# Routing of a soft mixture of experts: layer norm's gamma and beta moved from GpSimd into VectorE's normalisation

## The chip, the cores and the metric

One core of one Trainium2 chip. The metric is the device time of one execution in microseconds, median over runs.

## What is computed

Two layers on `x` (16 batches of 256 rows of 256 numbers, fp32): attention over a context and a feed-forward part, then a second attention and a soft mixture of 16 experts with 16 slots each. The change lies in the last part only, in the front of it:

```
xn = _layernorm(x, ln_gamma, ln_beta)      # (x - mu) * rsqrt(var + LN_EPS) * gamma + beta
x_unit = _l2norm(xn, axis=-1)
mu_unit = _l2norm(mu, axis=0)
logits = jnp.einsum('bnd,des->bnes', x_unit * scale, mu_unit)
dispatch = jax.nn.softmax(logits, axis=1)
combine = jax.nn.softmax(logits.reshape(B, N, E * S), axis=-1).reshape(B, N, E, S)
slot_in = jnp.einsum('bnd,bnes->besd', xn, dispatch)
```

The experts work on `slot_in`, and `combine` mixes what they give back.

## The kernel before, in words

The kernel is a row of stages with a barrier of all engines between them: `prologue` (keys and values), `attention0`, `ffn`, `attention1`, and in `moe` the stages `route`, `experts` and `combine`. Everything around `route` is left as it is. Each engine has its own program, in which the order is written out by hand; they are tied by semaphores alone. There is no scheduler.

`route` holds a batch as 128 partitions x 2 chunks (`NC`) x 256. Its body runs 17 times, unrolled (`every_batch`), and each engine is at another batch, so that in iteration f the following is done.

- **VectorE** (`batch` at L1684): normalise batch f+3 (`ln.normalise`, L346: two tensor_scalar into `xn`, recorded at L351), first maxima `top` of the logits (L1670), `disp_lo` of batch f-1 (L1692), inverse of the exponentials' sum `rinv` (L1675), first two `weight` (L1681), two `xT_lo` (L1665), second maxima, statistics of batch f+4 (L331, L334), inverse length of f+2 (L1660), second `rinv` and `weight`.
- **GpSimd** (L1768): `split_x(f)`, which makes `xaS_lo` (L1765); `affine(f+3)`, which makes `xg` from `xn` and gamma (L1746) and `xa` from `xg` and beta (L1752); `lengths(f+2)` (L1758, L1761); `inverse_deviation(f+4)`, which makes `var_eps` and `rstd` (L340, L343).
- **ScalarE** (L1623): `unit(f+1)`, which scales two rows of `xa` into `xu` (L1602), `disp_hi` (L1630), first exponentials (L1614), `xT_hi` (L1608), `square(f+2)` (L1596), second exponentials, `round_x(f+1)` into `xaS_hi` (L1621), then the copies `comb` (L1643) and `slots` (L1645) of batch f-1.
- **TensorE** (L1561): first logits of f (L1538), transposes of the first `weight` of f-1 (L1547), transposes of `xu` of f+1 (L1528), second logits, transposes of the second `weight`, and `slot_inputs` of f-1 (L1557), which waits for `disp_lo` and `xaS_lo`.

Logits, weights and dispatch are fp32 split into a high and a low part (`_hi`, `_lo`). `xn`, `xg`, `xu` and the logits' banks exist once, `xa` three times (`XR = 3`, L1470), so `affine(f)` waits until `xu` and `xaS_lo` of batch f-3 have been made.

Ahead of the batches stands a start in which the vectors `mu` are normalised (`mu_sq`, `mu_diag`, `mu_unit`, `mu_hi`, `mu_lo`, L1709 to L1731), mixed with the normalisation of batches 0, 1 and 2. gamma, beta and the scale are loaded at the stage's beginning; `affine(0)` and `mu_diag` wait for them.

Of the kernel before, what the change touches and what calls it, by code (L numbers as in the profile page):

```python
# [19 lines left out]
ALU = mybir.AluOpType  # L20
# [6 lines left out]
P = 128  # L27
B = 16
N = 256
NC = N // P  # L30
D = 256
# [18 lines left out]
def at_least(eng, sem, value):  # L50

    if not isinstance(value, int) or value > 0:
        eng.wait_ge(sem, value)


def wait_apart(eng, sem, value):

    at_least(eng.engine, sem, value)
    if not isinstance(value, int):
        eng.engine.sem_inc(eng.ticks, 1)  # L64
# [244 lines left out]
def x_rows(st, b, q):  # L309

    return st.x[:, bass.ds(b, 1), q, :].rearrange("p b e -> p (b e)")
# [1136 lines left out]
def route(nc, d, st):  # L1448
# [7 lines left out]
    with ExitStack() as stack:  # L1456
        m = Memory(nc, stack, "route")
# [9 lines left out]
        half = m.sb("half", [P, NC])  # L1467
        ln = LayerNorm(nc, m, st)
        xg = m.sb("xg", [P, NC, D])
        XR = 3  # L1470
        xa = [m.sb(f"xa{i}", [P, NC, D]) for i in range(XR)]
        sq = m.sb("sq", [P, D])
        sumsq, length, length_min, inv_length = (m.sb(n, [P, NC]) for n in ("sumsq", "length", "length_min", "inv_length"))
# [14 lines left out]
        in_, expert_in = m.sem("small_in"), m.sem("expert_in")  # L1488
        const_ready, mu_step, mu_psum, mu_ready = m.sem("const_ready"), m.sem("mu_step"), m.sem("mu_psum"), m.sem("mu_ready")
        mu_pow = m.sem("mu_pow")  # L1490
        xg_ready, xa_ready, sumsq_ready = m.sem("xg_ready"), m.sem("xa_ready"), m.sem("sumsq_ready")
        len_ready, lmin_ready, inv_ready, xu_ready = m.sem("len_ready"), m.sem("lmin_ready"), m.sem("inv_ready"), m.sem("xu_ready")
        xas_hi, xas_ready = m.sem("xas_hi"), m.sem("xas_ready")
        xt_psum, xt_hi, xt_lo = m.sem("xt_psum"), m.sem("xt_hi"), m.sem("xt_lo")
# [7 lines left out]
        def every_batch(eng, body):  # L1502
            for f in range(B + 1):
                body(f)
# [83 lines left out]
        @block.scalar  # L1588
        def _(act):
            def square(f, i):  # L1590

                act.wait_ge(xa_ready, f + 1)
                for q in range(NC):
                    at_least(act, sumsq_ready, NC * f + q)
                    at_least(act, len_ready, f)
                    nc.scalar.activation(sq[:, :], xa[f % XR][:, q, :], ACT.Square, accum_out=sumsq[:, q:q + 1]).then_inc(sumsq_ready, 1)  # L1596

            def unit(f, i):
                act.wait_ge(inv_ready, f + 1)
                at_least(act, xt_psum, DC * f)  # L1600
                for q in range(NC):
                    nc.scalar.mul(xu[:, q, :], xa[f % XR][:, q, :], inv_length[:, q:q + 1]).then_inc(xu_ready, 1)  # L1602

            def transposed_x(f, i):
                for c in range(DC):
                    act.wait_ge(xt_psum, DC * f + c + 1)
                    at_least(act, l_psum, 2 * (f - 1))
                    nc.scalar.copy(xT[i][0][:, c, :], x_bank[c][:, 0:N]).then_inc(xt_hi, 1)  # L1608

            def exponentials(f, k):  # L1610
                act.wait_ge(top_ready, 2 * f + k + 1)
                at_least(act, weight_ready, 4 * (f - 1) + 2 * k + 2)
                for r in range(2):
                    nc.scalar.activation(ex[k][:, r, :], l_bank[k][:, r * ES:(r + 1) * ES], ACT.Exp,  # L1614
                                         bias=top[k][:, r:r + 1], accum_out=rsum[k][:, r:r + 1]).then_inc(ex_ready, 1)

            def round_x(f, i):

                at_least(act, i_psum, f - 1)
                act.wait_ge(xa_ready, f + 1)  # L1620
                nc.scalar.copy(xaS[i][0][:, :, :], xa[f % XR][:, :, :]).then_inc(xas_hi, 1)  # L1621

            def batch(f):  # L1623
                g = f - 1
                if f + 1 < B:
                    unit(f + 1, 0)
                if f > 0:
                    act.wait_ge(t_psum, 2 * g + 1)
                    at_least(act, i_psum, g)
                    nc.scalar.copy(disp[0][:, :, :], t_bank[0][:, :].rearrange("p (q n) -> p q n", q=NC)).then_inc(disp_hi, 1)  # L1630
                if f < B:
                    exponentials(f, 0)
                if f + 1 < B:
                    transposed_x(f + 1, (f + 1) % 2)
                if f + 2 < B:
                    square(f + 2, 0)
                if f < B:
                    exponentials(f, 1)
                if f + 1 < B:
                    round_x(f + 1, (f + 1) % 2)  # L1640
                if f > 0:
                    act.wait_ge(t_psum, 2 * g + 2)
                    nc.scalar.copy(st.comb[:, :, g, :], t_bank[1][:, :].rearrange("p (j n) -> p j n", j=EC)).then_inc(comb_stored, 1)  # L1643
                    act.wait_ge(i_psum, g + 1)
                    nc.scalar.copy(st.slots[:, :, g, :], i_bank[:, :].rearrange("p (c n) -> p c n", c=DC)).then_inc(slots_stored, 1)  # L1645

            square(0, 0)
            unit(0, 0)
            transposed_x(0, 0)
            square(1, 1)  # L1650
            round_x(0, 0)
            every_batch(act, batch)

        @block.vector
        def _(dve):
            def invert_length(f):

                dve.wait_ge(lmin_ready, f + 1)
                at_least(dve, xu_ready, NC * f)
                nc.vector.reciprocal(inv_length[:, :], length_min[:, :]).then_inc(inv_ready, 1)  # L1660
# [23 lines left out]
            def batch(f):  # L1684
                g = f - 1
                if f + 3 < B:
                    ln.normalise(dve, f + 3, xg_ready, 1)
                if f < B:
                    maxima(f, 0)
                if f > 0:  # L1690
                    dve.wait_ge(disp_hi, g + 1)
                    nc.vector.tensor_tensor(disp[1][:, :, :], t_bank[0][:, :].rearrange("p (q n) -> p q n", q=NC),  # L1692
                                            fp32_of(disp[0][:, :, :]), ALU.subtract).then_inc(disp_lo, 1)
                if f < B:
                    invert(f, 0)
                    weigh(f, 0)
                if f + 1 < B:
                    transposed_x(f + 1, (f + 1) % 2)
                if f < B:
                    maxima(f, 1)  # L1700
                if f + 4 < B:
                    ln.statistics(dve, f + 4)
                if f + 2 < B:
                    invert_length(f + 2)
                if f < B:
                    invert(f, 1)
                    weigh(f, 1)
# [2 lines left out]
            ln.statistics(dve, 0)  # L1710
            dve.wait_ge(mu_psum, 1)
            nc.vector.tensor_copy(mu_sum[:, :], i_bank[:, 0:EC]).then_inc(mu_step, 1)
            ln.normalise(dve, 0, xg_ready, 1)
            ln.statistics(dve, 1)

            dve.wait_ge(mu_pow, 2)
            nc.vector.reciprocal(mu_inv[:, :], mu_max[:, :]).then_inc(mu_step, 1)
            dve.wait_ge(mu_step, 3)
            dve.wait_ge(in_, 48)
            for j in range(EC):  # L1720
                last = nc.vector.tensor_scalar(mu_diag[:, j, :], st.ident[:, :], mu_inv[:, j:j + 1], scale[:, 0:1],
                                               ALU.mult, ALU.mult)
            last.then_inc(mu_step, 1)
            ln.normalise(dve, 1, xg_ready, 1)
            dve.wait_ge(mu_psum, 2)
            nc.vector.tensor_tensor(mu_unit[:, :, :], mu_raw[:, :, :], l_bank[0][:, 0:ES].unsqueeze(1).to_broadcast([P, DC, ES]),
                                    ALU.mult).then_inc(mu_step, 1)
# [4 lines left out]
            ln.statistics(dve, 2)  # L1732
            invert_length(0)
            transposed_x(0, 0)
            ln.normalise(dve, 2, xg_ready, 1)
            ln.statistics(dve, 3)
            invert_length(1)
            every_batch(dve, batch)
# [1 line left out]
        @block.gpsimd  # L1740
        def _(pool):
            poolt = Ticking(pool, m.sem("pool_ticks"))
            def affine(f, i):
                wait_apart(poolt, ln.ready, NC * f + NC)
                wait_apart(poolt, xa_ready, f)
                nc.gpsimd.tensor_tensor(xg[:, :, :], ln.xn[:, :, :], gamma[:, :].unsqueeze(1).to_broadcast([P, NC, D]),  # L1746
                                        ALU.mult).then_inc(xg_ready, 1)
                wait_apart(poolt, xg_ready, f + 1)

                wait_apart(poolt, xu_ready, NC * (f - 2))  # L1750
                wait_apart(poolt, xas_ready, f - 2)
                nc.gpsimd.tensor_tensor(xa[f % XR][:, :, :], xg[:, :, :], beta[:, :].unsqueeze(1).to_broadcast([P, NC, D]),  # L1752
                                        ALU.add).then_inc(xa_ready, 1)

            def lengths(f):
                wait_apart(poolt, sumsq_ready, NC * f + NC)
                wait_apart(poolt, lmin_ready, f)
# [10 lines left out]
            def batch(f):  # L1768
                if f < B:
                    split_x(f, f % 2)  # L1770
                if f + 3 < B:
                    affine(f + 3, 0)
                if f + 2 < B:
                    lengths(f + 2)
                if f + 4 < B:
                    ln.inverse_deviation(pool, f + 4)
# [6 lines left out]
            nc.gpsimd.tensor_tensor(mu_norm[:, :], mu_sum[:, :], half[:, 0:EC], ALU.pow).then_inc(mu_pow, 1)  # L1783
            wait_apart(poolt, mu_pow, 1)
            nc.gpsimd.tensor_scalar(mu_max[:, :], mu_norm[:, :], NORM_EPS, None, ALU.max).then_inc(mu_pow, 1)
            wait_apart(poolt, in_, 48)
            affine(0, 0)
            ln.inverse_deviation(pool, 1)
            lengths(0)
            affine(1, 1)  # L1790
            lengths(1)
            ln.inverse_deviation(pool, 2)
            affine(2, 0)
            ln.inverse_deviation(pool, 3)
            every_batch(pool, batch)

# [338 lines left out]
```

## Time and profile before

| | |
|---|---|
| median of 3 runs | 1199.65 us (1196.87, 1199.65, 1201.66) |
| the profiled execution | 1201.5 us, its span 1199.7 us |
| busy over the span | TensorE 1020.2 us (85%), VectorE 883.1 (74%), ScalarE 751.3 (63%), GpSimd 470.3 (39%) |
| `route` in the span | from about 957 to 1110 us |

Busy shares over the whole span mix stages with different limits. The rows further down come from the stretch of `route`; times there are microseconds from the span's first instruction, and a row's columns are start, length, engine, line, operation, what is written and from what, its shape and count; in brackets stands how long the engine had been idle before it and who ended that.

### The profile page before, as it was taken

How to read it: one execution, taken by the hardware profiler on the slowest of the kernel's cores; microseconds unless marked ns; L12 is line 12 of the kernel's file. 1: busy time of each engine (PE TensorE's matmuls, PEld its weight loads, DVE VectorE, ACT ScalarE, POOL GpSimd, SP SyncE). 2: the span in 40 equal slices, each digit the busy share in tenths (PEclk: the TensorE clock that was granted, in tenths of full speed). 3: DMA queues.
4: the chain of work that ended last, by engine and by line, in shares of the span. 5: the costliest groups of instructions: out<-in, count | busy, mean ns of one | idle time of the engine just before them, and what ended most of it. 6: DMA issues, size and time to landing. Idle time of an engine off the chain costs nothing. (4 is left out here: it accounts for less than half of the span.)

```text
span 1199.7 us, 27786 instructions
## 1 busy us (share of the span) xinstructions
PE 1020.2 (85%) x8021; PEld 977.4 (81%) x8021; DVE 883.1 (74%) x2261; ACT 751.3 (63%) x2515; POOL 470.3 (39%) x801
## 2 busy tenths in 40 slices
PE   6779999999999999799999947888888637777578
PEld 6679999999999998699999946787887627677567
DVE  3567767777776676677777747999998668986776
ACT  3467666666666666433333338999898527777774
POOL 0132232322323222112121126667676467663655
PEclk9889999999999999899999966999999959999789
DMA  7678970000000000100000035555556050000003
GB/s 216 152 134 218 145 122 0 0 0 0 0 0 0 0 0 1 32 1 0 0 0 0 0 109 150 154 157 164 154 152 171 13 110 2 1 2 1 1 18 122
DMA packets 72190, 75.04 MB, mean 63 GB/s; under 512 B 22608, under 2 KB 64436, under 8 KB 71988
## 3 DMA queue, kind: packets, MB, share of 16 engines
q1 hardware_dynamic: 71300, 73.52, 24.8%
q10 hardware_dynamic: 816, 0.66, 0.2%
q8 instruction: 32, 0.52, 0.2%
q14 instruction: 42, 0.34, 0.1%
HBM read 42.58 MB, written 31.54 MB: 62 GB/s over the span
## 5 line engine op out<-in xcount | busy, mean ns | idle before, releaser
L776 POOL TENSOR_TENSOR att_prob<-att_ex,att_rinv 128x308 f32<-128x308 f32 x128 | 89.9, 702 | 215.8 <-DVE att_rinv L679 202.4
L1059 ACT ACTIVATE att_ex<-att_s_bank,att_mx 128x77 f32<-128x77 f32 x512 | 143.1, 340 | 13.7 <-DVE att_mx L1127 12.2
L1346 ACT ACTIVATE ffn_hid<-ffn_h_bank,ffn_b 128x256 f32<-128x256 f32 x128 | 60.6, 474 | 125.3 <-DVE ffn_hT_lo L1377 65.3
L638 ACT ACTIVATE att_ex<-att_s_bank,att_mx 128x77 f32<-128x77 f32 x512 | 124.7, 332 | 11.5 <-DVE att_mx L669 11.4
L646 ACT ACTIVATE att_qT<-att_q_bank 128x256 f32<-128x256 f32 x128 | 49.1, 384 | 101.2 <-PE att_q_bank L496 100.2
L702 DVE TENSOR_TENSOR att_pT_lo<-att_t_bank,att_pT_hi 128x512 fp32r<-128x512 f32 x128 | 88.3, 690 | 32.2 <-ACT att_pT_hi L616 31.8
L1203 POOL TENSOR_TENSOR att_prob<-att_ex,att_rinv 128x256 f32<-128x256 f32 x128 | 79.8, 623 | 77.2 <-DVE att_rinv L1142 77.1
L516 PE MATMUL att_s_bank<-att_keys,att_qT 128*128 128x154 f32 x512 | 94.9, 308 | 0.0
L616 ACT CAST att_pT_hi<-att_t_bank 128x512 fp32r<-128x512 f32 x128 | 74.9, 586 | 24.4 <-PE att_t_bank L526 19.3
L540 PE MATMUL att_o_bank<-att_pT_hi,att_vals_hi 128*128 128x256 f32 x256 | 83.0, 324 | 3.0 <-DVE att_oT_lo L683 2.0
L967 PE MATMUL att_s_bank<-att_ks,att_qs 100*128 100x154 f32 x256 | 53.2, 292 | 34.3 <-ACT att_ex L1059 17.4
L1317 PE MATMUL ffn_o_bank<-ffn_w_hi,ffn_hT_hi 128*128 128x256 f32 x256 | 74.3, 290 | 7.8 <-DVE ffn_hT_lo L1377 7.8
L683 DVE TENSOR_TENSOR att_oT_lo<-att_o_bank,att_oT_hi 128x256 fp32r<-128x256 f32 x128 | 54.3, 424 | 33.1 <-ACT att_oT_hi L651 29.6
L496 PE MATMUL att_q_bank<-att_xT_hi,att_wq_hi 128*128 128x256 f32 x256 | 75.6, 295 | 2.9 <-DVE att_xT_lo L662 2.9
L526 PE MATMUL att_t_bank<-all_ident,att_prob 128*128 128x128 f32 x512 | 76.5, 272 | 0.0
L1304 PE MATMUL ffn_h_bank<-ffn_xT_hi,ffn_w_hi 128*128 128x256 f32 x256 | 72.6, 283 | 3.5 <-DVE ffn_xT_lo L1364 3.5
L967 PEld LDWEIGHTS att_s_bank<-att_ks,att_qs 100*128 100x128 f32 x256 | 42.1, 205 | 40.4 <-DMA att_qs<-q_dram 31.2
L1127 DVE TENSOR_REDUCE att_mx<-att_s_bank 128x4 f32<-128x308 f32 x128 | 59.7, 466 | 20.3 <-PE att_s_bank L967 20.2
L516 PEld LDWEIGHTS att_s_bank<-att_keys,att_qT 128*128 128x128 f32 x512 | 73.2, 193 | 1.0
L496 PE MATMUL att_q_bank<-att_xT_hi,att_wq_lo 128*128 128x256 f32 x256 | 73.4, 287 | 0.0
L496 PE MATMUL att_q_bank<-att_xT_lo,att_wq_hi 128*128 128x256 f32 x256 | 73.1, 286 | 0.0
L1304 PE MATMUL ffn_h_bank<-ffn_xT_lo,ffn_w_hi 128*128 128x256 f32 x256 | 72.2, 282 | 0.0
(274 smaller groups left out, 4141.3 us busy)
## 6 DMA issues: line engine op xcount, KB each, us to landing
att_qs<-q_dram SPq DMA_DIRECT2D x96, 128.0 KB, 2.8
ks_dram<-att_zeros SPq DMA_DIRECT2D x16, 462.0 KB, 5.7
att_ks<-ks_dram SPq DMA_DIRECT2D x16, 462.0 KB, 4.9
all_x<-in_x SPq DMA_DIRECT2D x4, 1024.0 KB, 7.5
att_vd<-vd_dram SPq DMA_DIRECT2D x16, 256.0 KB
q_dram<-att_qT_hi SPq DMA_DIRECT2D x16, 256.0 KB, 2.1
q_dram<-att_qT_lo SPq DMA_DIRECT2D x16, 256.0 KB, 2.1
out<-comb_y SPq DMA_DIRECT2D x16, 256.0 KB, 2.1
```

Source lines behind the costliest of these rows:

```text
L496: last = nc.tensor.matmul(q_bank[c % 2][:, 0:N], wq[a][:, k, c * P:(c + 1) * P], xT[b][:, k, :], start=n == 0, stop=n == 5)
L516: last = nc.tensor.matmul(out, qT[c % 2][:, q * P:(q + 1) * P], keys[:, kc, h0:h0 + 2, :], start=first, stop=True)
L526: last = nc.tensor.transpose(t_bank[t % 2][:, h * N + q * P:h * N + (q + 1) * P], prob[:, q, (2 * t + h) * SK:(2 * t + h) * SK + P], st.id ...
L540: last = nc.tensor.matmul(o_bank[j % 2][:, 0:N], vals[a][:, v * P:(v + 1) * P], pT[t % 2][b][:, h * N:(h + 1) * N], start=t % PC == 0 and ...
L616: nc.scalar.copy(pT[t % 2][0][:, :], t_bank[t % 2][:, :]).then_inc(pt_hi, 1)
L638: last = nc.scalar.activation(ex[t % RING][:, r, :], s_bank[t % 2][:, r * SK:(r + 1) * SK], ACT.Exp, bias=mx[t % 2][:, r:r + 1])
L702: nc.vector.tensor_tensor(pT[t % 2][1][:, :], t_bank[t % 2][:, :], fp32_of(pT[t % 2][0][:, :]), ALU.subtract).then_inc(pt_lo, 1)
L776: nc.gpsimd.tensor_tensor(out, e, w, ALU.mult).then_inc(p_ready, 1)
L967: last = nc.tensor.matmul(s_bank[t % 2][:, q * PAIR:(q + 1) * PAIR], qs[i][0:ROWS, t, q * P:(q + 1) * P], ks[i][0:ROWS, t // 4, t % 4, :, ...
L1059: last = nc.scalar.activation(ex[t % RING][:, r, :], s_bank[t % 2][:, r * SK:(r + 1) * SK], ACT.Exp, bias=mx[t % 2][:, r:r + 1], **total)
L1203: nc.gpsimd.tensor_tensor(main, e[:, :, :, 0:MAIN], w.to_broadcast([P, NC, 2, MAIN]), ALU.mult).then_inc(p_ready, 1)
L1304: last = nc.tensor.matmul(h_bank[t % 4][:, 0:N], w1[a][:, k, t, :], xT[b][:, k, :], start=n == 0, stop=n == 5)
```

## The change

`affine` goes from GpSimd's program, and with it the semaphore `xa_ready`. VectorE's `ln.normalise` is replaced in this stage by a local `normalise`: for each chunk one scalar_tensor_tensor (x - mean) * gamma into `xg`, and then for each chunk a second, xg * rstd + beta, into `xa`. Who waited for `xa_ready` now waits for `ln.ready`, which the second one raises. `xa` has four buffers instead of three, so `normalise(f)` waits for `xu` and `xaS_lo` of batch f-4, where `affine(f)` waited for those of f-3. In ScalarE's program `unit` moves from the head of an iteration, for batch f+1, to behind `round_x`, for batch f+2, ahead of the copies `comb` and `slots`. VectorE now waits for gamma, beta and the scale before `normalise(0)`.

```
-        XR = 3
+        XR = 4
...
-                act.wait_ge(xa_ready, f + 1)
+                act.wait_ge(ln.ready, NC * f + NC)
...
             def batch(f):
                 g = f - 1
-                if f + 1 < B:
-                    unit(f + 1, 0)
...
                     round_x(f + 1, (f + 1) % 2)
+                if f + 2 < B:
+                    unit(f + 2, 0)
...
             round_x(0, 0)
+            unit(1, 0)
...
+            def normalise(f):
+                dve.wait_ge(ln.rstd_ready, f + 1)
+                at_least(dve, ln.ready, NC * f)
+                for q in range(NC):
+                    nc.vector.scalar_tensor_tensor(xg[:, q, :], x_rows(st, f, q), ln.mean_var[:, q, 0:1], gamma[:, :],
+                                                   ALU.subtract, ALU.mult).then_inc(xg_ready, 1)
+                at_least(dve, xu_ready, NC * (f - XR + 1))
+                at_least(dve, xas_ready, f - XR + 1)
+                for q in range(NC):
+                    dve.wait_ge(xg_ready, NC * f + q + 1)
+                    nc.vector.scalar_tensor_tensor(xa[f % XR][:, q, :], xg[:, q, :], ln.rstd[:, q:q + 1], beta[:, :],
+                                                   ALU.mult, ALU.add).then_inc(ln.ready, 1)
...
-                    ln.normalise(dve, f + 3, xg_ready, 1)
+                    normalise(f + 3)
...
-            ln.normalise(dve, 0, xg_ready, 1)
+            dve.wait_ge(in_, 48)
+            normalise(0)
...
-            def affine(f, i):
-                wait_apart(poolt, ln.ready, NC * f + NC)
-                wait_apart(poolt, xa_ready, f)
-                nc.gpsimd.tensor_tensor(xg[:, :, :], ln.xn[:, :, :], gamma[:, :].unsqueeze(1).to_broadcast([P, NC, D]),
-                                        ALU.mult).then_inc(xg_ready, 1)
-                wait_apart(poolt, xg_ready, f + 1)
-
-                wait_apart(poolt, xu_ready, NC * (f - 2))
-                wait_apart(poolt, xas_ready, f - 2)
-                nc.gpsimd.tensor_tensor(xa[f % XR][:, :, :], xg[:, :, :], beta[:, :].unsqueeze(1).to_broadcast([P, NC, D]),
-                                        ALU.add).then_inc(xa_ready, 1)
```

How the order moves, first on VectorE, from one `weight` pair over the normalisation to the next batch's `xT_lo`. Before:

```order
L1681 TENSOR_SCALAR route_weight<-route_ex,route_rinv 128x256 x2
L351 TENSOR_SCALAR route_xn<-all_x,route_mean_var,route_rstd 128x256 x2
L1670 TENSOR_REDUCE route_top<-route_l_bank 128x2
L1692 TENSOR_TENSOR route_disp_lo<-route_t_bank,route_disp_hi 128x512
L1675 RECIPROCAL route_rinv<-route_rsum 128x2
```

And changed:

```order
L1695 TENSOR_SCALAR route_weight<-route_ex,route_rinv 128x256 x2
L1661 SCALAR_TENSOR_TENSOR route_xg<-all_x,route_mean_var,route_gamma 128x256 x2
L1667 SCALAR_TENSOR_TENSOR route_xa<-route_xg,route_rstd,route_beta 128x256 x2
L1684 TENSOR_REDUCE route_top<-route_l_bank 128x2
L1706 TENSOR_TENSOR route_disp_lo<-route_t_bank,route_disp_hi 128x512
L1689 RECIPROCAL route_rinv<-route_rsum 128x2
```

Two instructions have become four, at the same place. On GpSimd, one iteration from `rstd` to the next `rstd`, before:

```order
L343 TENSOR_TENSOR route_rstd<-route_var_eps,all_minus_half 128x2
L1765 TENSOR_TENSOR route_xaS_lo<-route_xa,route_xaS_hi 128x512
L1746 TENSOR_TENSOR route_xg<-route_xn,route_gamma 128x512
L1752 TENSOR_TENSOR route_xa<-route_xg,route_beta 128x512
L1758 TENSOR_TENSOR route_length<-route_sumsq,route_half 128x2
L1761 TENSOR_SCALAR route_length_min<-route_length 128x2
L340 TENSOR_SCALAR route_var_eps<-route_mean_var 128x2
```

And changed:

```order
L343 TENSOR_TENSOR route_rstd<-route_var_eps,all_minus_half 128x2
L1767 TENSOR_TENSOR route_xaS_lo<-route_xa,route_xaS_hi 128x512
L1760 TENSOR_TENSOR route_length<-route_sumsq,route_half 128x2
L1763 TENSOR_SCALAR route_length_min<-route_length 128x2
L340 TENSOR_SCALAR route_var_eps<-route_mean_var 128x2
```

The two products and sums with gamma and beta are gone; `xaS_lo` stays right behind `rstd`. On ScalarE, from the second exponentials of an iteration to the first of the next, before:

```order
L1614 ACTIVATE route_ex,route_rsum<-route_l_bank,route_top 128x256 x2
L1621 CAST route_xaS_hi<-route_xa 128x512
L1643 COPY moe_comb<-route_t_bank 128x2x256
L1645 COPY moe_slots<-route_i_bank 128x2x256
L1602 ACTIVATE route_xu<-route_xa,route_inv_length 128x256 x2
L1630 CAST route_disp_hi<-route_t_bank 128x512
```

And changed:

```order
L1614 ACTIVATE route_ex,route_rsum<-route_l_bank,route_top 128x256 x2
L1621 CAST route_xaS_hi<-route_xa 128x512
L1602 ACTIVATE route_xu<-route_xa,route_inv_length 128x256 x2
L1643 COPY moe_comb<-route_t_bank 128x2x256
L1645 COPY moe_slots<-route_i_bank 128x2x256
L1628 CAST route_disp_hi<-route_t_bank 128x512
```

`xu` of the same batch now comes ahead of two copies instead of behind them.

## Rows read from the trace of the kernel before

**Rows 1.** Stretch 984 to 1081 us: length, then busy us (instructions), clock, DMA

```profile
984.00:1081.00 97.00, 69.46 (x547) 64.54 (x547) 86.50 (x216) 73.78 (x238) 67.90 (x84) 0.98 0.01 1
```

**Rows 2.** Who waited for whom, 990 to 1079 us: total, times, longest

```profile
ACT route_ex L1614 <- DVE route_top L1670: 20.2, 22, 1.3
PE route_x_bank L1528 <- ACT route_xu L1602: 18.1, 10, 1.8
```

**Rows 3.** Order in time, VectorE: one batch, and `top` of batches 0 and 12

```profile
984.08 0.68 DVE L1670 TENSOR_REDUCE route_top<-route_l_bank 128x2 f32<-128x512 f32 x1
...
1023.01 1.59 DVE L351 TENSOR_SCALAR route_xn<-all_x,route_mean_var,route_rstd 128x256 f32<-128x256 f32 x2
...
1024.52 0.68 DVE L1670 TENSOR_REDUCE route_top<-route_l_bank 128x2 f32<-128x512 f32 x1
...
1026.29 0.17 DVE L1675 RECIPROCAL route_rinv<-route_rsum 128x2 f32<-128x2 f32 x1 [0.49 <-ACT route_ex L1614]
...
1026.49 1.27 DVE L1681 TENSOR_SCALAR route_weight<-route_ex,route_rinv 128x256 f32<-128x256 f32 x2
...
1027.67 0.75 DVE L1665 TENSOR_TENSOR route_xT_lo<-route_x_bank,route_xT_hi 128x256 fp32r<-128x256 f32 x2
...
1028.34 0.68 DVE L1670 TENSOR_REDUCE route_top<-route_l_bank 128x2 f32<-128x512 f32 x1
...
1081.21 0.68 DVE L1670 TENSOR_REDUCE route_top<-route_l_bank 128x2 f32<-128x512 f32 x1
```

**Rows 4.** Order in time, GpSimd, the same batch

```profile
1022.18 0.79 POOL L343 TENSOR_TENSOR route_rstd<-route_var_eps,all_minus_half 128x2 f32<-128x2 f32 x1
1022.86 1.27 POOL L1765 TENSOR_TENSOR route_xaS_lo<-route_xa,route_xaS_hi 128x512 fp32r<-128x512 f32 x1
...
1026.05 1.29 POOL L1752 TENSOR_TENSOR route_xa<-route_xg,route_beta 128x512 f32<-128x512 f32 x1
```

**Rows 5.** Order in time, VectorE, near the stage's end

```profile
1089.54 0.69 DVE L1692 TENSOR_TENSOR route_disp_lo<-route_t_bank,route_disp_hi 128x512 fp32r<-128x512 f32 x1 [1.35 <-ACT route_disp_hi L1630]
...
1090.66 0.62 DVE L1681 TENSOR_SCALAR route_weight<-route_ex,route_rinv 128x256 f32<-128x256 f32 x2
1091.19 0.75 DVE L1665 TENSOR_TENSOR route_xT_lo<-route_x_bank,route_xT_hi 128x256 fp32r<-128x256 f32 x2
```

**Rows 6.** Order in time, the start: VectorE's `mu` and GpSimd's `xa`

```profile
957.09 0.69 DVE L1709 TENSOR_TENSOR route_mu_sq<-all_raw 128x512 f32<-128x512 f32 x1 [1.01 <-PEq L98]
...
968.56 1.22 DVE L1729 CAST route_mu_hi<-route_mu_unit 128x512 fp32r<-128x512 f32 x1
969.57 1.32 POOL L1752 TENSOR_TENSOR route_xa<-route_xg,route_beta 128x512 f32<-128x512 f32 x1
969.81 1.63 DVE L1731 TENSOR_TENSOR route_mu_lo<-route_mu_unit,route_mu_hi 128x512 fp32r<-128x512 f32 x1
```

**Rows 7.** VectorE: two rows of the prologue; by line, ns min/median/max, first and last

```profile
8.96 0.76 DVE L275 SCALAR_TENSOR_TENSOR pro_wk_lo<-pro_w_raw,pro_wk_hi 128x256 fp32r<-128x256 f32 x2 [0.24 <-ACT pro_wk_hi L240]
9.64 0.89 DVE L278 TENSOR_TENSOR pro_wv_lo<-pro_w_raw,pro_wv_hi 128x128 fp32r<-128x128 f32 x2
...
L1373 DVE CAST ffn_hT_hi<-ffn_hid x128: 263/293/1254, 502.0 to 695.4; 128x256 fp32r<-128x256 f32 x128
...
L1681 DVE TENSOR_SCALAR route_weight<-route_ex,route_rinv x64: 340/352/1003, 986.0 to 1106.3; 128x256 f32<-128x256 f32 x64
...
L351 DVE TENSOR_SCALAR route_xn<-all_x,route_mean_var,route_rstd x32: 399/410/1357, 959.8 to 1080.9; 128x256 f32<-128x256 f32 x32
```

**Rows 8.** Order in time, the start: VectorE and, last, GpSimd

```profile
963.49 2.65 DVE L1721 TENSOR_SCALAR route_mu_diag<-all_ident,route_mu_inv,route_scale 128x128 f32<-128x128 f32 x2 [1.91 <-DMA route_scale<-in_L_ffn_scale]
967.20 0.74 DVE L351 TENSOR_SCALAR route_xn<-all_x,route_mean_var,route_rstd 128x256 f32<-128x256 f32 x2 [1.05 <-POOL route_rstd L343]
...
979.49 0.30 DVE L334 BATCH_NORM_AGGREGATE route_mean_var<-route_stats 128x2 f32<-128x6 f32 x2
...
981.44 0.22 POOL L340 TENSOR_SCALAR route_var_eps<-route_mean_var 128x2 f32<-128x2 f32 x1
```

More of the change, by code:

```diff
@@ L1490, in route @@
         mu_pow = m.sem("mu_pow")
-        xg_ready, xa_ready, sumsq_ready = m.sem("xg_ready"), m.sem("xa_ready"), m.sem("sumsq_ready")
+        xg_ready, sumsq_ready = m.sem("xg_ready"), m.sem("sumsq_ready")
         len_ready, lmin_ready, inv_ready, xu_ready = m.sem("len_ready"), m.sem("lmin_ready"), m.sem("inv_ready"), m.sem("xu_ready")
@@ L1619, in round_x @@
                 at_least(act, i_psum, f - 1)
-                act.wait_ge(xa_ready, f + 1)
+                act.wait_ge(ln.ready, NC * f + NC)
                 nc.scalar.copy(xaS[i][0][:, :, :], xa[f % XR][:, :, :]).then_inc(xas_hi, 1)
@@ L1718, in _ @@
             dve.wait_ge(mu_step, 3)
-            dve.wait_ge(in_, 48)
             for j in range(EC):
@@ L1723, in _ @@
             last.then_inc(mu_step, 1)
-            ln.normalise(dve, 1, xg_ready, 1)
+            normalise(1)
             dve.wait_ge(mu_psum, 2)
@@ L1734, in _ @@
             transposed_x(0, 0)
-            ln.normalise(dve, 2, xg_ready, 1)
+            normalise(2)
             ln.statistics(dve, 3)
@@ L1770, in batch @@
                     split_x(f, f % 2)
-                if f + 3 < B:
-                    affine(f + 3, 0)
                 if f + 2 < B:
@@ L1785, in _ @@
             nc.gpsimd.tensor_scalar(mu_max[:, :], mu_norm[:, :], NORM_EPS, None, ALU.max).then_inc(mu_pow, 1)
-            wait_apart(poolt, in_, 48)
-            affine(0, 0)
             ln.inverse_deviation(pool, 1)
             lengths(0)
-            affine(1, 1)
             lengths(1)
             ln.inverse_deviation(pool, 2)
-            affine(2, 0)
             ln.inverse_deviation(pool, 3)
```

## The prediction

> **What bounds the kernel now.** Only the routing stage is touched, and the first view to read is the table of stretches: from 984 to 1081 us, while twelve batches go by, VectorE is busy 86.50 of 97.00 us, TensorE 69.46, ScalarE 73.78 and GpSimd 67.90, at a granted clock of 0.98 [rows 1]. The highest share is only a hint. The second view, who waited for whom in 990 to 1079 us, shows which engine the others wait for: TensorE waits 18.1 us for `xu` in 10 waits of up to 1.8, ScalarE 20.2 us for VectorE's maxima in 22 [rows 2]. The third, VectorE's order in time, gives the verdict. A batch takes (1081.21 - 984.08) / 12 = 8.09 us, and in the batch shown VectorE goes from one instruction to the next with one idle piece of any size, 0.49 us before `rinv`, which waits for ScalarE's exponentials of the maxima that VectorE has just made [rows 3]. No maximum waits for TensorE. So a batch lasts as long as VectorE's instructions from start to start, and TensorE's wait for `xu` is slack.
>
> Two of VectorE's spacings are longer than the work in them. The two `xn` begin at 1023.01, but `top` only at 1024.52; GpSimd's `xaS_lo` runs from 1022.86 to 1024.13 [rows 3, 4]. The first pair of `weight` begins at 1026.49 and `xT_lo` at 1027.67, 1.18 later; GpSimd's `xa` runs from 1026.05 to 1027.34 [rows 3, 4]. Without a large GpSimd instruction beside it the same pair takes 1091.19 - 1090.66 = 0.53 us [rows 5]. In both places VectorE comes second and stands until GpSimd is through.
>
> **The sum, per batch.** Three edits matter.
>
> (1) GpSimd's two 128x512 instructions (`xg`, and `xa` of 1.29 us [rows 4]) go. GpSimd's own time is not on the path. What is on it is the collision of `xa` with `weight`: 1.18 - 0.53 = 0.65 us less.
>
> (2) VectorE's two `xn` become four scalar_tensor_tensor of 128x256. The price of one: the two in the prologue begin at 8.96 and what follows them at 9.64, so 0.34 each, one lasting 0.42; their scalar is a constant [rows 7]. Here it is a column of 128 numbers. Among one-input instructions of 128x256 the median is 293 ns with no such scalar, 352 with one, 410 with two [rows 7], so I add 0.06: 0.40 from start to start (lower bound 0.34; the upper one is a rival below).
>
> Where they stand matters more. `normalise` waits for `rstd`, GpSimd's instruction right ahead of `xaS_lo`; `rstd` ends at 1022.97, `xn` starts at 1023.01, `xaS_lo` had started at 1022.86 [rows 3, 4]. The change keeps this order, so the first of the four again meets `xaS_lo`. Does an instruction with two SBUF inputs stand still too? `mu_lo` (128x512, two SBUF inputs) took 1.63 us beside GpSimd's `xa` and ended at 971.44, 0.55 after it; `mu_sq`, of the same shape, took 0.69 alone [rows 6]. So yes, and what comes after the block is about the work itself, 0.28 for 256 columns. From the end of `xaS_lo` to the start of `top` I get 0.28 + 3 x 0.40 - 0.08 (the next one starts that much before the last ends: `xT_lo` ends at 1028.42, `top` starts at 1028.34 [rows 3]) = 1.40 us. Before it is 1024.52 - 1024.13 = 0.39 [rows 3, 4]. That is 1.01 us more.
>
> (3) ScalarE scales `xu` of two batches on ahead of the `comb` and `slots` copies. TensorE gets it nearly a microsecond sooner, and I cost this at nothing: what hides it is VectorE, since no maximum waits for TensorE. Between the second exponentials of a batch and the first of the next ScalarE has the same five instructions in either order, and in mid-stage it then waits for `top` anyway [rows 2]. At the end of the stage, where ScalarE's chain is the path (VectorE waits 1.35 us for `disp_hi` [rows 5]), the count is again the same. If VectorE's cover were gone, the price would be that of rival B. The fourth buffer makes `normalise` wait only for batch f-1, done a batch ago: nothing.
>
> Net per batch: +1.01 - 0.65 = +0.36 us. Twelve batches lie between `top` of batch 0 and of batch 12: +4.3 us. The `weight` of batch 12 still saves its 0.65.
>
> **The start.** The chain up to `top` of batch 0 is serial. `normalise(0)` must now wait for gamma and beta, which come at about 963.5 (that is when `mu_diag` could start): four instructions with the wait for their end 1.7, statistics 1.0, `rstd` 1.1 give `normalise(1)` at 967.3, against 967.20 [rows 8]: +0.1. It takes 0.9 more than two `xn`. `mu_hi` (1.22, of which about 0.43 is work, by 293 ns for half the columns at two a cycle) and `mu_lo` (1.63 against 0.69) lose their collisions [rows 6, 7]: -1.7. `normalise(2)`: +0.9. `var_eps` of batch 3 starts at 981.44 though its statistics ended at 979.79, because `xg` and `xa` of batch 2 stand ahead [rows 8]: -1.6. `normalise(3)`: +1.0, as above. Sum -0.4 us.
>
> **Total:** 4.3 - 0.65 - 0.4 = +3.3 us. Those are rounded up; with 0.393 for 0.40 it is +3.0, which I take. The profiled execution took 1201.5 us (span 1199.7), so it would be 1204.5; it lies 1.85 above the median of the runs, 1199.65, so the forecast is **1202.6 us**, 0.25% more: no change. 0.5%, or 6 us, is about what a measurement of this kernel can tell from none.
>
> The sum is steep in one number: 36 of the instructions lie in the twelve periods and about 15 in the start, so 0.01 us on each is 0.5 us. At the lower bound of 0.34 the total is +0.3 us. The Trainium skill's "VectorE: DVE Perf Modes", section on the TRN2 errata, gives an SBUF instruction 58 + FD cycles of 0.96 GHz, 327 ns here; by that rule the sum would be about -0.4 us. The prologue's row has 0.34 from start to start and 0.42 for one, and the measurement decides.
>
> **Rivals.** *A, no collision.* Every collision that I used has a one-input instruction or a tensor_tensor in it; no row shows a scalar_tensor_tensor beside GpSimd. If it runs on, `top` starts 4 x 0.40 = 1.6 after the first, against 1.51 before: +0.1 - 0.65 = -0.55 a batch, 12 times, -1.0 more in the start: about -9 us, 1191. TensorE and ScalarE could follow (72% and 76% busy now [rows 1]). Against it: `mu_lo`. The skill's "SBUF — State Buffer", section on who interferes with whom, says that any VectorE instruction with two SBUF inputs contends with a GpSimd one that reads SBUF; `mu_lo` agrees. 9%.
>
> *B, TensorE's wait was the path.* If a batch turns on `xu`, putting it ahead of two copies (some 0.95 us) saves 0.95 in each of 14 batches: 1199.65 - 13 = 1186. Against it: `top` never waits for TensorE [rows 3]. 3%.
>
> *C, slower: each of the four costs its full length.* They wait on semaphores of their own engine (`xa` for `xg`). If each such wait empties VectorE, the spacing is 0.42 + 0.06 + 0.04 = 0.52 instead of 0.393: 51 x 0.127 = +6.5 us on top, 1209. It counts as slower from 0.46 on (3.0 + 51 x 0.06 = 6). For it: nothing here shows two-input instructions with a column scalar back to back. Against it: `xa` of a half waits for the instruction before the last one, which has ended by then. 13%.
>
> That the change does not do what it says is no case: the order of instructions shows all three moves.
>
> **Chances and range.** The forecast mechanism has 75%, A 9, B 3, C 13. Its own range is +0.3 to +3.0 us with the spread of the runs shown (1196.87 to 1201.66, -2.8 and +2.0), some 1197 to 1205. A tenth of each side is left out beyond: the range reaches towards A and into C, 1194.5 to 1208.5. The forecast case falls past +6 us in some 3 of 100, past -6 in 1. So faster 0.13 (A, B and 1), slower 0.16 (C and 3), within 0.5% the other 0.71.
>
> **What would show it.** In the steady stretch: period 8.45 us (8.09 now); `xaS_lo` start a little before the first `xg`, which lasts about 1.4 us, the other three 0.48 at 0.39 spacing; `weight` at 0.35 everywhere; TensorE's wait for `xu` down to about half, with a new one for `disp_lo`; `top` of batch 0 at about 983.6. A first `xg` of 0.48 beside `xaS_lo` makes A right and me wrong; a maximum that waits for TensorE, or a batch shorter than 8.0, as well; three later ones spaced at 0.5, C.

## The result and the profile after

The changed kernel takes 1203.97 us (median of 20 runs, 1199.65 to 1211.44), the kernel before 1199.35 us (20 runs, 1194.66 to 1206.13): a ratio of 1.0035, 95% interval 1.002 to 1.005. That is 0.35% or 4.2 us more (2.4 to 6.0), within the 0.5% that the forecast calls no change; it said +3.0. The profiled execution has a span of 1201.9 us.

The same stretch as in [rows 1], in the changed kernel: its length, then busy us and instructions of TensorE, its weight loads, VectorE, ScalarE and GpSimd, then clock and DMA.

```profile
984.00:1081.00 97.00, 71.97 (x541) 64.33 (x541) 86.92 (x231) 71.16 (x231) 34.79 (x57) 0.98 0.01 1
```

GpSimd has lost half of its busy time. VectorE is as busy as before, while fewer batches go by in the same 97 us. Who waited for whom in 990 to 1079 us, against [rows 2]:

```profile
POOL route_length L1760 <- ACT route_sq L1596: 46.9, 10, 4.7
ACT route_ex L1614 <- DVE route_top L1684: 23.8, 21, 2.1
...
PE route_i_bank L1557 <- DVE route_disp_lo L1706: 10.9, 11, 1.1
...
PE route_x_bank L1528 <- ACT route_xu L1602: 8.4, 10, 0.8
```

TensorE's wait for `xu` is less than half of what it was, and a wait for VectorE's `disp_lo` has come in its place. ScalarE waits longer for the maxima. TensorE and ScalarE still wait for VectorE; GpSimd, with little left to do, waits for ScalarE's squares. VectorE's order in time over one batch, with the rows of GpSimd that matter, against [rows 3, 4]:

```profile
1022.31 0.71 POOL L343 TENSOR_TENSOR route_rstd<-route_var_eps,all_minus_half 128x2 f32<-128x2 f32 x1
1022.33 0.62 DVE L1695 TENSOR_SCALAR route_weight<-route_ex,route_rinv 128x256 f32<-128x256 f32 x2
...
1022.99 1.27 POOL L1767 TENSOR_TENSOR route_xaS_lo<-route_xa,route_xaS_hi 128x512 fp32r<-128x512 f32 x1
1023.06 1.88 DVE L1661 SCALAR_TENSOR_TENSOR route_xg<-all_x,route_mean_var,route_gamma 128x256 f32<-128x256 f32 x2
...
1024.86 0.87 DVE L1667 SCALAR_TENSOR_TENSOR route_xa<-route_xg,route_rstd,route_beta 128x256 f32<-128x256 f32 x2
1025.65 0.68 DVE L1684 TENSOR_REDUCE route_top<-route_l_bank 128x2 f32<-128x512 f32 x1
...
1027.42 0.17 DVE L1689 RECIPROCAL route_rinv<-route_rsum 128x2 f32<-128x2 f32 x1 [0.49 <-ACT route_ex L1614]
...
1027.62 0.62 DVE L1695 TENSOR_SCALAR route_weight<-route_ex,route_rinv 128x256 f32<-128x256 f32 x2
...
1028.15 0.75 DVE L1679 TENSOR_TENSOR route_xT_lo<-route_x_bank,route_xT_hi 128x256 fp32r<-128x256 f32 x2
```

Read three distances here. `xaS_lo` starts 0.07 us ahead of the first `xg` and ends at 1024.26; `top` starts 1.39 later (0.39 before, 1.40 forecast). The four new instructions follow each other by 0.40: the two `xa` start at 1024.86 and `top` at 1025.65. From `weight` to `xT_lo` it is 0.53 instead of 1.18. Before, `top` to `xT_lo` took 3.15 us, now 2.50. One more distance is easy to miss: from the second `weight` pair (1022.33) to the first `xg` (1023.06) it is 0.73, where a pair alone takes 0.53. VectorE waits 0.20 us there for GpSimd's `rstd`, too little to be printed as idle time. It did so before as well, and the forecast did not need it.

The durations (ns min/median/max) show that one of the two long instructions of a batch is gone and the other has stayed. `weight`, whose longest was 1003, has no long one any more; in the normalisation the longest was 1357 for `xn` [rows 7] and is 1491 for the first `xg`:

```profile
L1661 DVE SCALAR_TENSOR_TENSOR route_xg<-all_x,route_mean_var,route_gamma x32: 472/481/1491, 963.1 to 1083.6; 128x256 f32<-128x256 f32 x32
...
L1695 DVE TENSOR_SCALAR route_weight<-route_ex,route_rinv x64: 344/352/356, 985.4 to 1109.3; 128x256 f32<-128x256 f32 x64
```

The ends of the twelve batches, and where gamma and beta arrive:

```profile
963.13 0.88 DVE L1661 SCALAR_TENSOR_TENSOR route_xg<-all_x,route_mean_var,route_gamma 128x256 f32<-128x256 f32 x2 [2.56 <-DMA route_scale<-in_L_ffn_scale]
...
983.40 0.68 DVE L1684 TENSOR_REDUCE route_top<-route_l_bank 128x2 f32<-128x512 f32 x1
...
1084.82 0.68 DVE L1684 TENSOR_REDUCE route_top<-route_l_bank 128x2 f32<-128x512 f32 x1
...
1110.28 0.69 DVE L1706 TENSOR_TENSOR route_disp_lo<-route_t_bank,route_disp_hi 128x512 fp32r<-128x512 f32 x1 [0.63 <-ACT route_disp_hi L1628]
```

A batch takes (1084.82 - 983.40) / 12 = 8.45 us, against 8.09. From the constants' arrival to the first `top` it is 20.27 us, against 984.08 - 963.49 = 20.59. From the `top` of batch 12 to the last `disp_lo` it is 25.46; in the trace before the last `disp_lo` starts at 1107.31, 26.10 after its `top`. The stage therefore changes by -0.32, +4.29 and -0.64, +3.33 us in all. In the start these rows stand against [rows 6, 8]:

```profile
965.89 0.60 DVE L1735 TENSOR_SCALAR route_mu_diag<-all_ident,route_mu_inv,route_scale 128x128 f32<-128x128 f32 x2
...
969.24 0.43 DVE L1743 CAST route_mu_hi<-route_mu_unit 128x512 fp32r<-128x512 f32 x1
969.70 0.69 DVE L1745 TENSOR_TENSOR route_mu_lo<-route_mu_unit,route_mu_hi 128x512 fp32r<-128x512 f32 x1
...
979.76 0.22 POOL L340 TENSOR_SCALAR route_var_eps<-route_mean_var 128x2 f32<-128x2 f32 x1 [2.80 <-DVE route_mean_var L334]
```

`mu_diag`, `mu_hi` and `mu_lo` took 2.65, 1.22 and 1.63 us before, with GpSimd's `xg` and `xa` beside them.

### The profile page after: what moved, and what is told of

Same layout as the page of the kernel before. It is cut to its first block and busy times, and to the rows that moved or that the text cites. A ratio compares the mean times of both kernels' runs of the same rounds, so it can differ in the third digit from the quotient of the medians.

```text
span 1201.9 us, 27769 instructions
## 1 busy us (share of the span) xinstructions
PE 1025.3 (85%) x8021; PEld 978.9 (81%) x8021; DVE 887.2 (74%) x2293; ACT 751.1 (62%) x2515; POOL 427.8 (36%) x769
```

## Experiments

All ratios are to the kernel before, timed in turn with it on the same chip; "batch" is the mean distance of `top` over the steady batches in the run's own trace. The changed kernel was not timed again beside the experiments, and the chips differ, so it is compared by ratios. A second measure leaves the timing noise out: the us from the constants' arrival to the start of the last `disp_lo`, in the one trace of each kernel.

| before | changed | exp. 1 | exp. 2 | exp. 3 | exp. 4 | exp. 5 | exp. 6 | exp. 7 |
|---|---|---|---|---|---|---|---|---|
| 143.82 | 147.15 | 134.16 | 144.37 | 147.16 | 134.65 | 134.27 | 130.23 | 131.31 |

**1. Start `xaS_lo` late.** In the changed kernel GpSimd's `batch` gets one wait:

```
                 if f < B:
+                    if f + 3 < B:
+                        wait_apart(poolt, ln.ready, NC * (f + 3) + NC)
                     split_x(f, f % 2)
```

> The changed kernel, but GpSimd starts xaS_lo of batch f only when VectorE's normalisation of batch f+3 has ended. Collision theory (the first xg of a batch lasts 1.49 us only because xaS_lo holds it up): the first xg falls to 0.48 us, the batch from 8.45 to about 7.44 us, the start loses 1.0 more, in all -13 us against the changed kernel, about 1191 us, 0.7% under the kernel before. Rival 1 (the time goes in waiting for rstd or for semaphores, not in the collision): the batch stays at 8.4 us and the time at 1204. Rival 2 (xaS_lo comes too late for TensorE's slot_inputs): the first xg falls, but maxima wait for TensorE and the batch stays above 7.9 us.

Measured: 1192.76 us, ratio 0.992 (0.9902 to 0.9938), batch (1073.83 - 984.42) / 12 = 7.45 us. VectorE and GpSimd in time:

```profile
1027.54 0.88 DVE L1661 SCALAR_TENSOR_TENSOR route_xg<-all_x,route_mean_var,route_gamma 128x256 f32<-128x256 f32 x2
...
1028.34 0.88 DVE L1667 SCALAR_TENSOR_TENSOR route_xa<-route_xg,route_rstd,route_beta 128x256 f32<-128x256 f32 x2
...
1029.13 0.68 DVE L1684 TENSOR_REDUCE route_top<-route_l_bank 128x2 f32<-128x512 f32 x1
1029.30 1.29 POOL L1767 TENSOR_TENSOR route_xaS_lo<-route_xa,route_xaS_hi 128x512 fp32r<-128x512 f32 x1 [1.79 <-DVE route_xa L1667]
1029.73 0.68 DVE L1706 TENSOR_TENSOR route_disp_lo<-route_t_bank,route_disp_hi 128x512 fp32r<-128x512 f32 x1
```

The same four instructions, the same semaphores, no GpSimd instruction beside them: 1.59 us to `top` instead of 2.59. The collision is worth 1.00 us per batch and 13.0 us in the stage, as expected. Moving it away costs nothing, since `top` and `disp_lo` (one input in PSUM) run beside `xaS_lo` at 0.68. Both rivals fall.

**2. The same wait in the kernel before**, ahead of the same call, with `affine(f + 3)` behind it as it was.

> The kernel before with the same single edit: xaS_lo of batch f waits for xn of batch f+3. Theory: GpSimd's three large instructions only move later; xn loses its collision, but the first weight pair then meets xg and xa, one instruction each, as mu_diag did, so the batch stays at 8.1 to 8.2 us (8.09 before) and the time within 2 us of the kernel before. Rival (delaying xaS_lo is a gain in itself, without moving gamma and beta): xn loses 0.85 us and weight loses nothing more, the batch falls to about 7.3 us and the time by 10 us.

Measured: 1202.56 us, ratio 1.0002 (0.9985 to 1.0019), batch (1077.21 - 979.60) / 12 = 8.13 us. The `xn` are free, and most of what they gain is lost in the first `weight` pair, one instruction behind `xg` and one behind `xa`:

```profile
1027.76 0.73 DVE L351 TENSOR_SCALAR route_xn<-all_x,route_mean_var,route_rstd 128x256 f32<-128x256 f32 x2
...
1028.57 1.27 POOL L1765 TENSOR_TENSOR route_xaS_lo<-route_xa,route_xaS_hi 128x512 fp32r<-128x512 f32 x1 [0.85 <-DVE route_xn L351]
...
1029.59 0.69 DVE L1692 TENSOR_TENSOR route_disp_lo<-route_t_bank,route_disp_hi 128x512 fp32r<-128x512 f32 x1 [0.50 <-ACT route_disp_hi L1630]
1029.80 1.30 POOL L1746 TENSOR_TENSOR route_xg<-route_xn,route_gamma 128x512 f32<-128x512 f32 x1
...
1030.72 1.90 DVE L1681 TENSOR_SCALAR route_weight<-route_ex,route_rinv 128x256 f32<-128x256 f32 x2
...
1031.18 1.29 POOL L1752 TENSOR_TENSOR route_xa<-route_xg,route_beta 128x512 f32<-128x512 f32 x1
```

From `xn` to `top` it is 0.65 us instead of 1.51, and from `weight` to `xT_lo` 1.82 instead of 1.18: 0.64 of the 0.86 is lost there. Between `top` and `rinv` another 0.34 goes (2.11 for 1.77), because VectorE now waits 0.50 us for ScalarE's `disp_hi`, which the expectation did not have. So the late `xaS_lo` is no gain by itself. The two large GpSimd instructions behind it are the larger part of the reason, ScalarE's order the rest; no run takes away one of the two alone.

**3. `xu` back at its old place, three buffers.** The changed kernel with

```
-        XR = 4
+        XR = 3
...
+                if f + 1 < B:
+                    unit(f + 1, 0)
...
-                if f + 2 < B:
-                    unit(f + 2, 0)
...
-            unit(1, 0)
```

> The changed kernel with xu scaled at the head of the iteration again and three buffers of xa: only gamma and beta have moved. Theory (VectorE's spacing is the path): nothing, batch 8.45 us and time within 1.5 us of the changed kernel, while TensorE's wait for xu in the steady stretch goes back up from 8 to about 18 us. Rival B (TensorE's wait for xu is on the path): about 0.5 us or more per batch, 7 us slower than the changed kernel, 1211.

Measured: 1205.15 us, ratio 1.0032 (1.0013 to 1.005), batch (1082.80 - 981.42) / 12 = 8.45 us. The wait for `xu` shows that it did change something:

```profile
PE route_x_bank L1528 <- ACT route_xu L1602: 18.3, 10, 1.9
```

The stage is as long as in the changed kernel (147.16 and 147.15 us). Moving gamma and beta gives the whole result; the earlier `xu` and the fourth buffer give nothing here.

**4. Half of the normalisation.** Mean and gamma are left out of the computation, so that two of the four instructions remain, `xa` from `x`, `rstd` and beta:

```
-                for q in range(NC):
-                    nc.vector.scalar_tensor_tensor(xg[:, q, :], x_rows(st, f, q), ln.mean_var[:, q, 0:1], gamma[:, :],
-                                                   ALU.subtract, ALU.mult).then_inc(xg_ready, 1)
...
-                    dve.wait_ge(xg_ready, NC * f + q + 1)
-                    nc.vector.scalar_tensor_tensor(xa[f % XR][:, q, :], xg[:, q, :], ln.rstd[:, q:q + 1], beta[:, :],
+                    nc.vector.scalar_tensor_tensor(xa[f % XR][:, q, :], x_rows(st, f, q), ln.rstd[:, q:q + 1], beta[:, :],
```

> The changed kernel with the normalisation cut to two of its four instructions: the subtraction of the mean and the product with gamma are left out. Theory (the batch is VectorE's instructions end to end, 0.40 us for each of these): the first of the two is still blocked behind xaS_lo, the batch falls by 2 x 0.40 to 7.66 us and the start by 3 us: -12.5 us against the changed kernel, about 1191.5. Rival (something else, ScalarE or TensorE, is within 0.3 us of being the path): the batch falls to no less than 8.1 us and the time by under 7 us.

Measured: 1192.32 us, ratio 0.9919 (0.9894 to 0.9944), batch (1073.34 - 981.38) / 12 = 7.66 us, constants to the first `top` 981.38 - 964.19 = 17.19 us, 3.1 less. Two instructions less are 0.79 us less per batch: 0.40 each, all of it on the path, and 12.5 us in the stage, as expected.

**5. Late `xaS_lo` and `xu` at its old place.** Edits 1 and 3 together, but with four buffers: with three, VectorE's `normalise(f+3)` would wait for `xaS_lo` of batch f and GpSimd for `normalise(f+3)`, by the waits in the code; this was not run.

> The late xaS_lo kernel with xu scaled at the head of the iteration again (four buffers of xa are needed here and stay). At 7.45 us per batch TensorE gets xu 0.95 us later and ends slot_inputs some 0.4 us after the point at which it could begin the next logits. Theory: these logits are needed only at the next batch's first maxima, over 2.5 us later, so the batch stays at 7.45 us and the time within 1.5 us of the late kernel (ratio to the kernel before 0.992). Rival: with VectorE faster, TensorE's wait for xu is the path: batch 7.7 us or more, 3 us or more slower than the late kernel.

Measured: 1188.75 us, ratio 0.9904 (0.9877 to 0.9931), batch (1070.35 - 980.86) / 12 = 7.46 us. TensorE waits 18.0 us for `xu` again in 10 waits (990 to 1070 us; 8.6 in experiment 1), and the batch is as long as in experiment 1, the stage within 0.11 us. The ratio's interval takes in the ratio of experiment 1. What the fourth buffer does is to make the late `xaS_lo` possible.

**6. Late `xaS_lo`, and the normalisation behind the first maxima.** On top of edit 1, in VectorE's `batch`:

```
-                if f + 3 < B:
-                    normalise(f + 3)
                 if f < B:
                     maxima(f, 0)
+                if f + 3 < B:
+                    normalise(f + 3)
```

> The late xaS_lo kernel with VectorE's normalisation moved behind the first maxima, so that ScalarE's exponentials run beside it and VectorE does not idle 0.49 us for them. xaS_lo then starts when the normalisation ends and meets the first weight pair about 0.7 us later, which is blocked for some 0.5 us. Theory: 7.45 - 0.49 - 0.2 + 0.6, about 7.3 us per batch, 1 to 2 us faster than the late kernel (about 0.991 of the kernel before). Rival (the pair does not collide): 6.9 us per batch, 6 us faster. Rival (TensorE, which gets xaS_lo late, is the path): 7.8 us or more, slower than the late kernel.

Measured: 1185.57 us, ratio 0.9877 (0.985 to 0.9904), batch (1064.45 - 993.16) / 10 = 7.13 us over batches 2 to 12. VectorE in time:

```profile
1021.65 0.69 DVE L1684 TENSOR_REDUCE route_top<-route_l_bank 128x2 f32<-128x512 f32 x1
...
1023.84 0.69 DVE L1706 TENSOR_TENSOR route_disp_lo<-route_t_bank,route_disp_hi 128x512 fp32r<-128x512 f32 x1
...
1024.00 1.29 POOL L1767 TENSOR_TENSOR route_xaS_lo<-route_xa,route_xaS_hi 128x512 fp32r<-128x512 f32 x1 [2.19 <-DVE route_xa L1667]
...
1024.61 0.17 DVE L1689 RECIPROCAL route_rinv<-route_rsum 128x2 f32<-128x2 f32 x1
1024.81 0.90 DVE L1695 TENSOR_SCALAR route_weight<-route_ex,route_rinv 128x256 f32<-128x256 f32 x2
1025.62 0.74 DVE L1679 TENSOR_TENSOR route_xT_lo<-route_x_bank,route_xT_hi 128x256 fp32r<-128x256 f32 x2
```

The idle piece ahead of `rinv` is gone. `weight` does meet `xaS_lo`, which has 0.48 us left when it starts, but loses only 0.28 (0.81 to `xT_lo` for 0.53), not 0.5 to 0.6. The expectation of 1 to 2 us under experiment 1 was a miss: the stage is 3.9 us shorter. The twelve distances of `top` give 2.7 of it (86.72 us for 89.41). The first `top` no longer stands behind `normalise(3)` and comes 16.54 us after the constants (977.73 - 961.19), against 984.42 - 965.15 = 19.27 in experiment 1, but 1.5 of these 2.7 us are given back behind the `top` of batch 12.

**7. The same order with `xaS_lo` at its old place.** Experiment 6 without its wait on GpSimd.

> The changed kernel with VectorE's normalisation behind the first maxima, xaS_lo at its old place. xaS_lo starts where it did; the maxima read PSUM and run beside it, so only the last 0.6 us of it block the first xg. Theory: first xg about 0.9 us, no idle piece before rinv, weight at 0.35 us, about 7.3 to 7.4 us per batch, 13 us faster than the changed kernel, like the late kernel without its wait (0.991 to 0.993 of the kernel before). Rival (a collision costs the whole of the GpSimd instruction wherever it meets): batch 8.0 us or more.

Measured: 1185.30 us, ratio 0.9883 (0.9853 to 0.9912), batch (1065.13 - 992.38) / 10 = 7.27 us.

```profile
1020.94 0.62 DVE L1695 TENSOR_SCALAR route_weight<-route_ex,route_rinv 128x256 f32<-128x256 f32 x2
1021.47 0.68 DVE L1684 TENSOR_REDUCE route_top<-route_l_bank 128x2 f32<-128x512 f32 x1
...
1021.59 1.28 POOL L1767 TENSOR_TENSOR route_xaS_lo<-route_xa,route_xaS_hi 128x512 fp32r<-128x512 f32 x1
...
1022.07 1.48 DVE L1661 SCALAR_TENSOR_TENSOR route_xg<-all_x,route_mean_var,route_gamma 128x256 f32<-128x256 f32 x2
...
1023.47 0.87 DVE L1667 SCALAR_TENSOR_TENSOR route_xa<-route_xg,route_rstd,route_beta 128x256 f32<-128x256 f32 x2
```

`top` takes its usual 0.68 beside `xaS_lo`, which has 0.80 us left when the first `xg` starts: the two `xg` take 1.40 to the next start for 0.79, 0.61 more. So a collision costs what is left of the GpSimd instruction, less some 0.2 us, and not the whole of it. The batch came as expected, the total did not: the stage is 15.8 us shorter than in the changed kernel, for 13 expected. Of the 1.18 us per batch, 0.39 is the shorter block and 0.56 the idle piece before `rinv` (`disp_lo` to `rinv` 0.60 for 1.16). Another 0.20 is the wait for `rstd`, which `top` now covers: 1020.94 to 1021.47, 0.53 us for 0.73.

Experiments 6 and 7 cannot be told apart by their times. Both beat the kernel before by 1.2% and the changed one by 1.5 to 1.6%. Neither order was tried in the kernel before, so how much of it needs gamma and beta on VectorE is not shown.

## Why the prediction was right

- **What bounds the batch: right.** In the steady stretch VectorE waits for no TensorE instruction in any of the traces, and two of its instructions less shorten the batch by their 0.79 us (experiment 4). Rival B, TensorE's wait for `xu`, is refuted: the wait went from 8.4 us back to 18.3 (experiment 3) with the batch at 8.45 both times.
- **(1) The `weight` collision, -0.65: right**, 1.18 to 0.53.
- **(2) Four instructions at 0.40 behind a block: right**, 1.39 us from the end of `xaS_lo` for 1.40. The price had been put together from an instruction with a constant scalar and from the steps between other instructions; experiment 4 finds 0.40 with no other view. The 0.393 that the total goes by has no row of its own; the two `xa` have 0.395. The block behind `xaS_lo` had been argued from `mu_lo`; experiment 1 shows it, 1.00 us. Rival A, no collision, is refuted by it. The Trainium skill ("SBUF — State Buffer", section on who interferes with whom) says that a VectorE instruction with two SBUF inputs contends with a GpSimd one that reads SBUF; the trace agrees, with 1.00 us for scalar_tensor_tensor. The formula of the Trainium skill's "VectorE: DVE Perf Modes", section on the TRN2 errata, would give an estimate of 0.33 us for the spacing; 0.40 was measured here.
- **Rival C, each at its full length: refuted.** They last 0.47 to 0.48 and start every 0.40, `xa` as `xg`, so waiting for the instruction before the last one costs nothing.
- **(3) The earlier `xu`, nothing: right** (experiment 3).
- **The start, -0.4: right**, -0.3, and in the two traces term by term: `normalise(1)` begins 0.09 us later after the constants (0.1 forecast) and takes 0.94 more (0.9), from the start of `mu_hi` to the statistics it is 1.74 less (1.7), `normalise(2)` takes 0.94 more (0.9), `var_eps` of batch 3 comes 1.57 sooner after the statistics' start (1.6), and from there to `top` it is 1.00 more (1.0).
- **The end of the stage, -0.65: right**, -0.64.

By the forecast's steps the stage grows by 3.0 to 3.3 us, by the trace by 3.3; the median moved by 4.6, the ratio gives 4.2 with an interval from 2.4 to 6.0. What lies between 3.3 and 4.2 is not settled, and needs no cause inside that interval. That the median and the forecast agree this closely is in part luck, at a spread of several us from run to run; that the parts agree is not. One thing that moves by itself: the constants arrive between 5.4 and 6.4 us after the stage's first VectorE instruction, 5.44 in the profile of the changed kernel and 6.40 in the one before, and 6.08 to 6.21 in experiments 1, 3 and 4. The two spans, 1199.7 and 1201.9, hold that difference of 1.0 us in the changed kernel's favour, 0.6 us that it starts the stage later, and 0.8 us less behind the last `disp_lo`; so they differ by 2.2 and not by 3.3.

Why does taking half of GpSimd's work away gain nothing? GpSimd's large instructions were never the path; they only held VectorE up twice per batch (its small `rstd` is waited for, 0.2 us, in both kernels). One of the two collisions went with the work, worth 0.65, and the work itself came to VectorE for 1.01 (a batch grew by 8.45 - 8.09 = 0.36). The collision that stayed was worth 1.00, and it stayed because `xaS_lo` comes right behind `rstd` in GpSimd's own program, while the normalisation waits for `rstd` by a semaphore: GpSimd starts 0.07 us ahead.

## What to carry to other kernels

Work that is taken from an engine with slack to the one that bounds must be weighed against the collisions that go with it, one by one, by start to start distances and not by busy time. Where a large GpSimd instruction follows directly on the one that releases a VectorE instruction of a kind that stood still here (tensor_scalar, cast, scalar_tensor_tensor or two-input tensor_tensor, all from SBUF), let the engine with slack wait. One such wait on GpSimd was worth 1.0 us per batch here, and nothing while the other large GpSimd instructions were still there. An order change that puts ready work into known waits (the normalisation behind the first maxima) took 15.8 us off the changed kernel's stage, where moving the work between engines had added 3.3.

## What had not been expected of the hardware

A VectorE instruction that is held up gets some 0.2 us of the block back: it loses 1.00 us where GpSimd has 1.20 left (the changed kernel), 0.61 of 0.80 (experiment 7), 0.28 of 0.48 (experiment 6), and in the kernel before `weight` lost 0.65 of 0.85 and `mu_lo` 0.94 of 1.08. Small GpSimd instructions held nothing up: the second `weight` pair of the changed kernel starts 0.02 us behind `rstd` and takes 0.62 us, as alone. The prediction took the two long blocks from rows and so had this in its numbers without naming it; the expectation of experiment 6 did not.

A pair of VectorE instructions can be held up twice: in experiment 2 the two `weight` took 1.90 us together for 0.62, one behind `xg` and one behind `xa`, since GpSimd's next instruction gets in between them. `mu_diag` in the kernel before, 2.65 us for two [rows 8], is the same, and takes 0.60 in the changed kernel, where GpSimd has nothing large beside it. The second `mu_diag` of the kernel before and GpSimd's `xa`, read alone:

```profile
964.73 1.42 DVE L1721 TENSOR_SCALAR route_mu_diag<-all_ident,route_mu_inv,route_scale 128x128 f32<-128x128 f32 x1
964.80 1.26 POOL L1752 TENSOR_TENSOR route_xa<-route_xg,route_beta 128x512 f32<-128x512 f32 x1
```

By its recorded start VectorE is 0.07 us ahead here, and stands all the same. So recorded starts as close as this do not tell who will stand, and the 0.07 us by which GpSimd leads in the steady batches is not shown to be what decides.
